# Three turns of tables for the expert sums, six row buffers, and scatters over 112 partitions

## Chip, cores and metric

The kernel runs on one core of a Trainium2 chip. The metric is device time in microseconds (us) for one execution; a time given as "the kernel's" is the median of several executions. All stretches and starts below are in us from the start of the profiled span.

## What is computed

One transformer layer over 2 x 1024 tokens of width 256: causal attention with rotary positions, a residual and a layer norm, then a mixture of experts with a shared expert, again a residual and a layer norm. The change touches only how the outputs of the routed experts come together with the rest. Cut to what matters:

```python
E, K, H, F = (64, 6, 256, 96);  CAP = 2 * (256 * K // E)          # 48 slots for each expert
def _routed_moe(x, topk_w, topk_ids, w_gate, w_up, w_down):
    order = jnp.argsort(topk_ids.reshape(-1));  se = flat_e[order];  tok = order // K
    pos = jnp.arange(Tn * K) - jnp.searchsorted(se, se, side='left')   # place within its expert
    valid = pos < CAP                                                   # later tokens are dropped
    buf = zeros((E, CAP + 1, H)).at[se, slot].set(x[tok])[:, :CAP]
    h = silu(einsum('ech,ehf->ecf', buf, w_gate)) * einsum('ech,ehf->ecf', buf, w_up)
    out = einsum('ecf,efh->ech', h, w_down)
    return segment_sum(out[se, pos] * valid * w, tok, num_segments=Tn)  # sum over a token's experts
x = layernorm(x + attention(x))
x = layernorm(x + routed_moe(x) + silu(x @ ws_gate) * (x @ ws_up) @ ws_down)
```

## The kernel before

**Attention and routing.** Up to about 990 us the kernel projects, attends and routes, tile by tile (16 tiles of 128 tokens). Every engine walks the same list of steps, `SEQ`, and waits on semaphores. For each tile the step `x1t` lets SyncE write zeros into the tile's rows of the sum tables (`blank_sums`, L576): all tables but the first, whose rows are written by step `sd` (L644), which stores the first layer norm's output plus the shared expert. The step `place` scatters each token's row into its six experts' slots (L729, GpSimd). Each expert has 64 slots (`HALF`) in `slot_rows`, of which at most 48 (`CAP`) are filled. SyncE also loads the experts' weights into 28 places (`HOMES`) as attention's memory comes free.

**Experts.** The 64 experts go in 32 pairs, one expert on partitions 0 to 63 and the other on 64 to 127, so that the slots in use are partitions 0 to 47 and 64 to 111. For pair `n` TensorE transposes the slots (L1038), multiplies by gate and up weights (L1048), transposes the hidden values (L1055) and multiplies by the down weights (L1062). ScalarE writes the result, times the routing weight of each slot, into row buffer `erow[n % EB]` (L879, `rows_out`), with `EB = 4`. GpSimd then issues one indirect DMA with an add (L742): each of the 128 partitions' rows of 1 KB is added to a row of the tables `sums` in HBM. An unused slot is directed to a spare row behind the tokens' rows.

**Tables and turns.** Two adds in flight must not touch the same row. So the two experts of a pair have a table each, and pairs alternate between two turns: `TURNS = 2`, `TABLES = 2 * TURNS = 4`. GpSimd issues pair `n` only when the pair `n - TURNS` has landed (`used(pool, erow_sent[n % TURNS], ...)`, L741), and ScalarE writes a row buffer again only when pair `n - EB` has landed (L878). ScalarE works in order, and `rows_out(n - 2)` stands behind `slots_in(n + 1)` and `gate_sig(n)`: a wait in it stops the inputs of later pairs too. The four pairs that have no place in `wexp` at first are loaded when `dn_ready` reaches 8, 12, 16 and 20 (L651), and the slots come in six chunks, the last three issued by ScalarE behind pairs 0, 6 and 12 (L892).

**Final sums.** When the last scatter of every turn has landed (L654), SyncE loads the tables, chunk by chunk (`FINAL = 8` chunks of 256 tokens, 256 KB for each chunk and table, L657). TensorE adds the tables of even chunks by matmuls with the identity (L1084), VectorE those of odd chunks by adds (L1340). Both wait for all tables of the chunk. VectorE then takes mean and variance (L1330, L1333), GpSimd the power (L750), ScalarE applies them (L899), and SyncE stores the chunk (L660).

Of the kernel before, what the change touches and what calls it, by code (L numbers as in the profile page):

```python
# [7 lines left out]
ALU = mybir.AluOpType  # L8
ACT = mybir.ActivationFunctionType
AX_X = mybir.AxisListType.X  # L10
F32 = mybir.dt.float32
# [4 lines left out]
P = 128  # L16
# [13 lines left out]
CAP = 2 * (256 * K // E)  # L30
PAIRS = E // 2
# [1 line left out]
SLOT_CUTS = (0, 2, 8, 14, 20, 26, PAIRS)  # L33
SLOT_CHUNKS = len(SLOT_CUTS) - 1
CHUNK_AT = {n: g for g, n in enumerate(SLOT_CUTS[:-1])}
EB = 4
TURNS = 2
TABLES = 2 * TURNS
HALF = P // 2
TOKENS = B * T  # L40
TABLE = TOKENS + P
# [4 lines left out]
FAR = 1.0e5  # L46
ABOVE, GONE = 1e30, -3e38
SLOTS = E * HALF
BLANKS = 4

UNITS = TILES * G
# [178 lines left out]
def build(nc, x, w_aq, w_ak, w_av, w_ao, gate_w, bias, w_gate, w_up, w_down, ws_gate, ws_up, ws_down,  # L230
# [4 lines left out]
    sums = nc.dram_tensor("sums", (TABLES * TABLE, M), F32, kind="Internal").ap()  # L235
# [3 lines left out]
    with ExitStack() as ctx:  # L239
        def sb(name, shape, dt, where=ctx):  # L240
            return where.enter_context(nc.sbuf_tensor(name, shape, dt))

        def sem(name):
            return ctx.enter_context(nc.semaphore(name))
# [6 lines left out]
        ones_bf = sb("ones_bf", [P, P], BF16)  # L251
        minus_half = sb("minus_half", [P, 1], F32)
        slots_left = sb("slots_left", [P, E], F32)
        row_base = sb("row_base", [P, PAIRS], F32)
        spare = sb("spare", [P, 1], F32)
        pool_cell = sb("pool_cell", [P, 1], F32)
        dve_cell = sb("dve_cell", [P, 1], F32)
# [90 lines left out]
        goal_u = sb("goal_u", [P, PAIRS], U32, exp)  # L348
        erow = sb("erow", [P, EB, M], F32, exp)
        exp.close()  # L350
# [85 lines left out]
        erow_ready = sem("erow_ready")  # L436
        erow_sent = [sem(f"erow_sent{n}") for n in range(TURNS)]
        fsum_added = sem("fsum_added")
# [60 lines left out]
        def used(eng, semaphore, n):  # L499

            if n > 0:
                eng.wait_ge(semaphore, n)
# [10 lines left out]
        def down_bank(n):  # L513
            return ring[:, n % 2, 0:M]
# [13 lines left out]
        def _(sp):  # L528
            def load_x(n):
                i = n % TILES  # L530
                sp.dma_start(x_sb[:, n % XB, :], xf[i * P:(i + 1) * P, :]).then_inc(x_loaded[n % XB], 16)

            load_x(0)
            for name in BLOCKS_IN_TURN:
                n = BLOCKS.index(name)
# [19 lines left out]
            def load_pair(n):  # L555
                k = n % HOMES
                for a, w in enumerate((w_gate, w_up)):
                    dst = wexp[:, k, 0:GATE_UP].rearrange("p (e a y) -> p e a y", e=2, a=2)[:, :, a, :]
                    sp.dma_start(dst, w[2 * n:2 * n + 2, :, :].rearrange("e (p c) f -> p e (c f)", c=MC)
                                 ).then_inc(experts_loaded[k], 16)  # L560
                sp.dma_start(wexp[0:F, k, GATE_UP:].rearrange("f (e m) -> f e m", e=2),
                             w_down[2 * n:2 * n + 2, :, :].rearrange("e f m -> f e m")
                             ).then_inc(experts_loaded[k], 16)
# [20 lines left out]
            for s in SEQ:  # L584
                if s[0] == "xt" and s[1] >= 1:
                    sp.wait_ge(xt_ready, s[1])
                    load_x(s[1] + 2)
                if s[0] == "xt" and 1 <= s[1] <= SLOTS // P // BLANKS:
                    n = s[1] - 1
                    sp.dma_start(slot_rows.rearrange("(p n) r -> p n r", p=P)[:, n * BLANKS:(n + 1) * BLANKS, :],  # L590
                                 blank[:, :].rearrange("p (a r) -> p a r", a=1).to_broadcast([P, BLANKS, ROW])
                                 ).then_inc(blank_stored, 16)
# [57 lines left out]
            for n in range(HOMES, PAIRS):  # L650
                sp.wait_ge(dn_ready, SLOT_CUTS[2] + 4 * (n - HOMES))  # L651
                load_pair(n)
            for n in range(TURNS):
                sp.wait_ge(erow_sent[n], 16 * (PAIRS // TURNS))  # L654
            for c in range(FINAL):
                for a in range(TABLES):
                    sp.dma_start(fsum[:, c, a, :], token_rows[a][:, c, :]).then_inc(fsum_loaded[c], 16)  # L657
# [7 lines left out]
        def _(pool):  # L665
            own = [0]

            def link(ins):

                own[0] += 1  # L670
                ins.then_inc(pool_own, 1)
                pool.wait_ge(pool_own, own[0])
# [3 lines left out]
                                    pattern=[[-1, P]], channel_multiplier=1))  # L676
# [7 lines left out]
                                    pattern=[[-1, P]], channel_multiplier=1))  # L684
# [3 lines left out]
                                    pattern=[[-1, P]], channel_multiplier=1))  # L688
# [6 lines left out]
            link(pool.memset(open_[:, :], ABOVE))  # L695
            link(pool.iota(slots_left[:, :], pattern=[[-HALF, E]], base=SLOTS, channel_multiplier=0,
                           allow_small_or_imprecise_dtypes=True))
            for e in range(2):
                link(pool.iota(row_base[e * HALF:(e + 1) * HALF, :], pattern=[[0, PAIRS // TURNS], [2 * TABLE, TURNS]],
                               base=e * TABLE, channel_multiplier=0, allow_small_or_imprecise_dtypes=True))  # L700
            link(pool.iota(spare[:, :], pattern=[[0, 1]], base=TOKENS, channel_multiplier=1,
                           allow_small_or_imprecise_dtypes=True))
# [2 lines left out]
            for s in SEQ:  # L705
                if s[0] == "proj" and s[2] != "V":

                    n = ROPE_AT[s[1:]]
# [14 lines left out]
                if s[0] == "place":  # L723
                    i = s[1]
                    if i == 0:
                        pool.wait_ge(blank_stored, 16 * (SLOTS // P // BLANKS))
                    pool.wait_ge(placed, i + 1)
                    for k in range(K):
                        pool.indirect_dma_start(  # L729
                            slot_rows[:, :], bass.IndirectOffsetOnAxis(ap=slot_u[:, i % 2, k:k + 1], axis=0),  # L730
                            row[:, i % 2, :], None, bounds_check=SLOTS - 1, oob_is_err=False
                        ).then_inc(scattered[i % 2], 16)
# [4 lines left out]
            for n in range(PAIRS):  # L737
                if n in CHUNK_AT:
                    pool.wait_ge(slots_known, CHUNK_AT[n] + 1)
                pool.wait_ge(erow_ready, n + 1)  # L740
                used(pool, erow_sent[n % TURNS], 16 * (n // TURNS))  # L741
                pool.indirect_dma_start(  # L742
                    sums[:, :], bass.IndirectOffsetOnAxis(ap=goal_u[:, n:n + 1], axis=0),
                    erow[:, n % EB, :], None, bounds_check=TABLES * TABLE - 1, oob_is_err=True, compute_op=ALU.add
                ).then_inc(erow_sent[n % TURNS], 16)


# [7 lines left out]
        def _(act):  # L755
# [9 lines left out]
            for s in SEQ:  # L765
                for name in HIGH_AT.get(s, []):
                    n = BLOCKS.index(name)
# [43 lines left out]
                if kind == "exp":  # L811
                    u, h = s[1:]
                    n = u * H + h
# [9 lines left out]
                if kind == "ptrans":  # L823
                    n = PT_AT[s[1:]]
# [47 lines left out]
            def rows_out(n):  # L872

                act.wait_ge(dn_ready, n + 1)
                if n in CHUNK_AT:
                    act.wait_ge(slots_known, CHUNK_AT[n] + 1)

                used(act, erow_sent[n % TURNS], 16 * ((n - EB) // TURNS + 1))  # L878
                act.activation(erow[:, n % EB, :], down_bank(n), ACT.Copy, scale=slot_w[:, n:n + 1]  # L879
                               ).then_inc(erow_ready, 1)  # L880

            for n in range(PAIRS + 2):
                if n == 0:
                    slots_in(0)
                if n + 1 < PAIRS:
                    slots_in(n + 1)
                if n < PAIRS:
                    gate_sig(n)
                if n >= 2:
                    rows_out(n - 2)  # L890
                if n in CHUNK_AT and 1 <= CHUNK_AT[n] < SLOT_CHUNKS - 2:
                    load_slots(CHUNK_AT[n] + 2)  # L892
# [196 lines left out]
        def _(dve):  # L1089
# [15 lines left out]
            def after(ins):  # L1105

                later(ins)
                settled()
# [5 lines left out]
            for s in SEQ:  # L1114
# [145 lines left out]
                if kind == "place":  # L1260
                    i = s[1]
                    read(dve, ("count", i))
                    with nc.allow_low_precision("at most one a tile"):
                        dve.tensor_tensor(taken[:, :], taken[:, :], chose[:, :], ALU.add)
                    after(dve.tensor_tensor(ahead[:, :], ahead[:, :], fits[:, :], ALU.mult))
                    after(dve.max(slot8[:, :], ahead[:, :]))
                    dve.tensor_scalar(slot_u[:, i % 2, :], slot8[:, :], -1.0, float(SLOTS), ALU.mult, ALU.add  # L1267
                                      ).then_inc(placed, 1)
# [110 lines left out]
```

## Time and profile before

| | us |
|---|---|
| median of 3 runs | 1127.45 (1126.43 to 1128.49) |
| the profiled execution: its time | 1126.55 |
| its span, first to last instruction | 1124.70 |
| start of the first scatter of the experts' sums | 1004.65 |
| start of the last scatter | 1085.84 |
| start of the first load of the tables | 1089.70 |
| start of VectorE's first add of the last chunk | 1115.49 |

The profiled execution is 0.90 us under the median. Of its time 1.85 us lies outside the span. Over the whole span TensorE is 90% busy, but that is an average over stages: in the last 120 us it is not, and the rows further down are read from these.

### The profile page before, as it was taken

Reading aid. Unit: us, or ns where it says so; the run is one execution under the profiler, and the core shown is the slowest. Engines: PE = TensorE matmul, PEld = TensorE weight load, DVE = VectorE, ACT = ScalarE, POOL = GpSimd, SP = SyncE. Lnnn points to the kernel's source line nnn. Section 1 sums busy time; section 2 is a strip of 40 time slices with the busy share of each in tenths; the row PEclk is TensorE's granted clock in tenths of the full one; section 3 lists DMA queues with packets and bytes.
Section 4 is the critical chain, followed back from the end, with each engine's and each line's share of the span. In section 5 each row is a group of like instructions: output and inputs, shape, how many; then the busy total and the mean of one; then the engine's idle time right before and its main releaser. Section 6 shows DMA issues by size and latency. Waiting matters only on the chain.

```text
span 1124.7 us, 16829 instructions
## 1 busy us (share of the span) xinstructions
PE 1017.0 (90%) x5312; PEld 731.9 (65%) x5312; DVE 562.6 (50%) x1533; ACT 518.7 (46%) x1147; POOL 363.4 (32%) x402
## 2 busy tenths in 40 slices
PE   6999998789999999999998899999999999657825
PEld 4888887566667776767666666777776676434512
DVE  5766765365554454443425675454535444323306
ACT  3333334454564556454543555464645645133312
POOL 6666665123322212103033313313021121035641
PEclk9999999799999999999999999999999999868868
DMA  7455233533321111111113323333211033968558
GB/s 230 163 180 183 105 117 108 163 91 106 95 63 62 53 56 49 38 43 51 34 44 98 101 80 95 112 104 100 65 39 52 26 92 91 245 178 175 80 100 315
DMA packets 99462, 117.57 MB, mean 105 GB/s; under 512 B 16065, under 2 KB 69173, under 8 KB 99376
## 3 DMA queue, kind: packets, MB, share of 16 engines
q1 hardware_dynamic: 76752, 87.65, 25.3%
q10 hardware_dynamic: 13408, 22.09, 6.5%
q0 software_dynamic: 9216, 6.76, 4.0%
q8 instruction: 44, 0.72, 0.3%
q14 instruction: 42, 0.34, 0.1%
HBM read 76.48 MB, written 53.35 MB: 115 GB/s over the span
## 4 chain that ended last, share of the span: by engine, by line
PE 75%; DMA 9%; DVE 6%; issue 4%; ACT 3%; SPq 2%; POOL 1%; ACTq 0%; POOLq 0%; DVEq 0%
PE o_ps L986 21%; PE s_ps L963 16%; PE ring L973 11%; PE ring L994 10%; DMA sums<-erow,goal_u 6%; PE s_ps L934 6%; PE ring L934 5%; PE s_ps L941 1%; SPq L657 1%; PE s_ps L966 1%; DVE neg_max L1150 1%; ACT probs L820 1%; DMA fsum<-sums 1%; PE o_ps L934 1%; PE ring L941 1%
## 5 line engine op out<-in xcount | busy, mean ns | idle before, releaser
L986 PE MATMUL o_ps<-pt,v 128*128 128x512 f32 x576 | 297.2, 598 | 3.9 <-DVE ot L1165 3.8
L828 ACT ACTIVATE pt<-ring 128x512 f32<-128x512 f32 x288 | 170.9, 594 | 252.1 <-PE ring L973 251.8
L963 PE MATMUL s_ps<-kt,qt_hi 128*128 128x512 f32 (+3 forms) x768 | 261.3, 422 | 3.5 <-issue 1.9
L1150 DVE TENSOR_REDUCE neg_max<-s_ps 128x1 f32<-128x128 f32 (+7 forms) x256 | 191.8, 753 | 135.8 <-PE s_ps L966 135.2
L820 ACT ACTIVATE probs<-s_ps,neg_max 128x128 f32<-128x128 f32 (+7 forms) x256 | 189.3, 740 | 110.2 <-DVE neg_max L1150 102.4
L718 POOL TENSOR_TENSOR qt_lo<-q_raw,qt_hi 128x512 fp32r<-128x512 f32 x64 | 81.2, 1270 | 474.1 <-ACT qt_hi L758 474.1
L963 PEld LDWEIGHTS s_ps<-kt,qt_hi 128*128 128x128 f32 x768 | 139.4, 194 | 79.4 <-issue 61.2
L973 PE MATMUL ring<-ident,probs 128*128 128x128 f32 x1152 | 176.2, 276 | 11.4 <-ACT probs L820 11.3
L973 PEld LDWEIGHTS ring<-ident,probs 128*128 128x128 f32 x1152 | 129.3, 142 | 56.8 <-issue 56.8
L963 PE MATMUL s_ps<-kt,qt_lo 128*128 128x512 f32 (+3 forms) x384 | 134.2, 350 | 0.0
L729 POOL DMA_INDIRECT slot_rows<-row,slot_u x96 | 94.5, 984 | 66.5 <-DVE slot_u L1267 39.7
L994 PE MATMUL ring<-wo,ot 128*128 128x256 f32 x512 | 113.1, 379 | 0.0
L994 PEld LDWEIGHTS ring<-wo,ot 128*128 128x128 f32 x512 | 97.1, 190 | 19.1 <-issue 6.7
L986 PEld LDWEIGHTS o_ps<-pt,v 128*128 128x128 f32 x576 | 87.8, 192 | 6.6 <-issue 6.4
L712 POOL TENSOR_TENSOR q_rot<-q_cos,q_sin 128x256 f32<-128x256 f32 x80 | 60.8, 760 | 63.0 <-DVE q_sin L1138 63.0
L963 PEld LDWEIGHTS s_ps<-kt,qt_lo 128*128 128x128 f32 x384 | 73.6, 192 | 8.3
L1165 DVE TENSOR_TENSOR ot<-o_ps,inv_row 128x512 f32<-128x512 f32 x64 | 44.1, 690 | 67.8 <-PE o_ps L986 62.7
L742 POOL DMA_INDIRECT sums<-erow,goal_u x32 | 49.3, 1542 | 48.0 <-ACT erow L879 25.2
L1173 DVE TENSOR_TENSOR y_sb<-ring,x_sb 128x256 f32<-128x256 f32 x16 | 6.8, 425 | 113.0 <-PE ring L994 113.0
L713 POOL TENSOR_TENSOR q_rot<-q_cos,q_sin 128x256 f32<-128x256 f32 x80 | 61.4, 768 | 0.0
L966 PE MATMUL s_ps<-causal_bf,ident_bf 128*128 128x128 bf16 x256 | 59.8, 233 | 0.0
L820 ACT ACTIVATION_READ_ACCUMULATOR probs<-s_ps,neg_max 128x1 f32 x256 | 50.4, 197 | 0.0
(182 smaller groups left out, 1283.7 us busy)
## 6 DMA issues: line engine op xcount, KB each, us to landing
q_rows<-q_out SPq DMA_DIRECT2D x64, 256.0 KB, 2.0
q_raw<-q_rows ACTq DMA_DIRECT2D x64, 256.0 KB, 2.7
inv_row<-inverses SPq DMA_DIRECT2D x64, 256.0 KB, 3.3
fsum<-sums SPq DMA_DIRECT2D x32, 256.0 KB, 6.9
sums<-blank SPq DMA_DIRECT2D x16, 384.0 KB, 2.8
wexp<-in_L_ffn_w_gate_dram SPq DMA_DIRECT2D x32, 192.0 KB, 3.9
wexp<-in_L_ffn_w_up_dram SPq DMA_DIRECT2D x32, 192.0 KB, 4.2
wexp<-in_L_ffn_w_down_dram SPq DMA_DIRECT2D x32, 192.0 KB, 5.0
```

The costliest lines, as they stand in the source:

```text
L713: pool.tensor_tensor(rot[:, :, 1, :], by_cos[:, :, 1, :], by_sin[:, :, 0, :], ALU.add).then_inc(rot_ready, 1)
L718: pool.tensor_tensor(qt_lo[:, u % 2, :], q_raw[:, u % QB, :], qt_hi[:, u % 2, :].bitcast(F32), ALU.subtract).then_inc(q_ready, 1)
L729: pool.indirect_dma_start(slot_rows[:, :], bass.IndirectOffsetOnAxis(ap=slot_u[:, i % 2, k:k + 1], axis=0), row[:, i % 2, :], None, bounds ...
L820: act.activation(probs[:, u % 2, h, 0:blocks(u) * P], s_ps[:, n % 2, score_cols(n)], ACT.Exp, bias=neg_max[:, n % 8:n % 8 + 1], accum_out= ...
L828: reader(act.activation(pt[:, n % PTB, :], bank(s), ACT.Copy), s)
L934: ins = pe.matmul(bank(s), (xt_hi, xt_lo)[xp][:, i % 2, c, :], (w_hi, w_lo)[wp][:, n, :, c, :], start=(c == 0 and xp == wp == 0), stop=(c ...
L963: pe.matmul(s_ps[:, n % 2, c + a:c + e], q[qp], k[kp][:, a:e], start=(qp == kp == 0), stop=(qp == 1 and not last))
L966: ins = pe.matmul(s_ps[:, n % 2, c + e - P:c + e], ident_bf[:, :], causal_bf[:, :], start=False, stop=True)
L973: ins = pe.transpose(bank(s)[:, h * P:(h + 1) * P], probs[:, u % 2, h, j * P:(j + 1) * P], ident[:, :])
L986: pe.matmul(o_ps[:, :], v_sb[i // NT][:, g, j, :], pt[:, n % PTB, :], start=(j == 0), stop=(j == blocks(u) - 1)).then_inc(pv_done, 1)
L994: ins = pe.matmul(bank(s)[:, 0:M], ot[:, h // H, (h % H) * P:(h % H + 1) * P], wo[:, h, :], start=(h == 0), stop=(h == G * H - 1))
L1150: dve.tensor_reduce(neg_max[:, n % 8:n % 8 + 1], s_ps[:, n % 2, score_cols(n)], AX_X, ALU.max, negate=True).then_inc(max_ready, 1)
```

## The change

`TURNS` goes from 2 to 3 and with it `TABLES` from 4 to 6; `EB` goes from 4 to 6. A pair's scatter covers 112 partitions, 0 to 111, in place of 128. The rest follows from it: `row_base` is rounded up to 33 columns so that its pattern repeats over three turns, and the wait ahead of the table loads counts each turn's own number of scatters (11, 11 and 10). Every loop over `TABLES` grows: `blank_sums` writes five tables in place of three, the blank of the spare rows six in place of four, the final loads are 48 in place of 32, TensorE adds six tables for each even chunk, and VectorE makes five adds in place of three for each odd one.

```diff
-EB = 4
-TURNS = 2
+EB = 6
+TURNS = 3
 TABLES = 2 * TURNS
...
 SLOTS = E * HALF
+USED = HALF + CAP
...
-        row_base = sb("row_base", [P, PAIRS], F32)
+        row_base = sb("row_base", [P, -(-PAIRS // TURNS) * TURNS], F32)
...
             for n in range(TURNS):
-                sp.wait_ge(erow_sent[n], 16 * (PAIRS // TURNS))
+                sp.wait_ge(erow_sent[n], 16 * len(range(n, PAIRS, TURNS)))
...
-                link(pool.iota(row_base[e * HALF:(e + 1) * HALF, :], pattern=[[0, PAIRS // TURNS], [2 * TABLE, TURNS]],
+                link(pool.iota(row_base[e * HALF:(e + 1) * HALF, :], pattern=[[0, -(-PAIRS // TURNS)], [2 * TABLE, TURNS]],
...
                 pool.indirect_dma_start(
-                    sums[:, :], bass.IndirectOffsetOnAxis(ap=goal_u[:, n:n + 1], axis=0),
-                    erow[:, n % EB, :], None, bounds_check=TABLES * TABLE - 1, oob_is_err=True, compute_op=ALU.add
+                    sums[:, :], bass.IndirectOffsetOnAxis(ap=goal_u[0:USED, n:n + 1], axis=0),
+                    erow[0:USED, n % EB, :], None, bounds_check=TABLES * TABLE - 1, oob_is_err=True, compute_op=ALU.add
                 ).then_inc(erow_sent[n % TURNS], 16)
...
-                used(act, erow_sent[n % TURNS], 16 * ((n - EB) // TURNS + 1))
+                used(act, erow_sent[(n - EB) % TURNS], 16 * ((n - EB) // TURNS + 1))
```

## Rows read from the trace of the kernel before

**Rows 1.** Chain that ended last, from 985 us on: shares by line.
```profile
by line: DMA sums<-erow,goal_u 49.7%; SPq L657 10.3%; issue 7.7%; DMA fsum<-sums 7.0%; ACT erow L879 4.5%; DMA slot_rows<-row,slot_u 3.0%; PE s_ps L1048 2.8%; DMA srow<-slot_rows 2.1%; POOL slot_rows L729 2.1%; POOL sums L742 1.7%; DVE fsum
```
**Rows 2.** Waits from 995 us on: who waited for whom, us in total, times, longest.
```profile
ACT erow L879 <- DMA sums<-erow,goal_u: 43.1, 24, 4.5
```
**Rows 3.** Timeline of GpSimd's scatters: start, us, instruction, idle before it.
```profile
1004.65 1.56 POOL L742 DMA_INDIRECT sums<-erow,goal_u  x1 [14.59 <-DVE dve_cell L1291]
...
1056.03 1.54 POOL L742 DMA_INDIRECT sums<-erow,goal_u  x1 [1.26 <-ACT erow L879]
...
1079.29 1.54 POOL L742 DMA_INDIRECT sums<-erow,goal_u  x1 [1.22 <-ACT erow L879]
...
1081.13 1.54 POOL L742 DMA_INDIRECT sums<-erow,goal_u  x1 [0.30 <-ACT erow L879]
1083.91 1.54 POOL L742 DMA_INDIRECT sums<-erow,goal_u  x1 [1.24 <-DMA sums<-erow,goal_u]
```
**Rows 4.** The chain again, in order: a scatter's time from its start to landing.
```profile
1015.05 6.86 DMA sums<-erow,goal_u
...
1033.49 5.66 DMA sums<-erow,goal_u
...
1079.29 3.81 DMA sums<-erow,goal_u
```
**Rows 5.** Timeline of the gate and up matmuls of single pairs, at either clock.
```profile
1007.37 0.88 PE L1048 MATMUL s_ps<-wexp,sxt 128*64 128x192 f32 x8
...
1009.09 0.88 PE L1048 MATMUL s_ps<-wexp,sxt 128*64 128x192 f32 x8
...
1022.87 1.55 PE L1048 MATMUL s_ps<-wexp,sxt 128*64 128x192 f32 x8 [3.06 <-issue]
...
1026.01 1.56 PE L1048 MATMUL s_ps<-wexp,sxt 128*64 128x192 f32 x8
```
**Rows 6.** DMA queues, 1004.6 to 1056: packets, MB, share of 16 engines (q0 is GpSimd's).
```profile
q0 software_dynamic: 2513, 2.30, 36.8%
q10 hardware_dynamic: 2329, 2.96, 18.8%
q1 hardware_dynamic: 3008, 2.36, 16.2%
```
**Rows 7.** The same for 1060.6 to 1083.9, where only scatters run.
```profile
q0 software_dynamic: 1449, 1.32, 52.2%
```
**Rows 8.** GpSimd's two kinds of scatter by line: duration ns min/median/max, first and last start.
```profile
L742 POOL DMA_INDIRECT sums<-erow,goal_u x32: 1532/1539/1570, 1004.7 to 1085.8; - x32
...
L729 POOL DMA_INDIRECT slot_rows<-row,slot_u x96: 967/972/1214, 253.0 to 989.1; - x96
```
**Rows 9.** Timeline of the final sums: issue of the loads, first use of some chunks.
```profile
1089.70 16.55 SPq L657 DMA_DIRECT2D fsum<-sums  x32
1095.86 9.47 PE L1084 MATMUL ring<-fsum,ident 128*128 128x512 f32 x16 [18.16 <-DMA fsum<-sums]
...
1104.69 0.69 DVE L1340 TENSOR_TENSOR fsum<-fsum 128x512 f32<-128x512 f32 x1 [0.37 <-DMA fsum<-sums]
...
1115.49 0.69 DVE L1340 TENSOR_TENSOR fsum<-fsum 128x512 f32<-128x512 f32 x1 [0.67 <-DMA fsum<-sums]
...
1117.09 0.69 DVE L1340 TENSOR_TENSOR fsum<-fsum 128x512 f32<-128x512 f32 x1
```
**Rows 10.** DMA from 1108 to 1115: all queues.
```profile
DMA packets 1494, 2.72 MB, mean 389 GB/s; under 512 B 169, under 2 KB 169, under 8 KB 1493
```
**Rows 11.** VectorE's waits for `inv_row`, 200 to 990: us in total, times, longest.
```profile
DVE ot L1165 <- DMA inv_row<-inverses: 3.5, 2, 2.5
```
**Rows 12.** Windows: PE, PEld, DVE, ACT, POOL busy, clock, DMA share, GB/s.
```profile
985.00:990.00 5.00, 0.40 (x2) 0.11 (x1) 0.48 (x2) 0.46 (x2) 3.83 (x4) 0.50 0.54 146
```

**Rows 13.** Windows of the scatters' stretch in which the clock was down, first and last of three.
```profile
1022.70:1027.80 5.10, 4.93 (x27) 3.16 (x27) 1.51 (x6) 1.84 (x8) 3.07 (x2) 0.50 0.45 56
...
1056.00:1060.60 4.60, 4.44 (x27) 2.74 (x27) 1.51 (x6) 1.89 (x8) 3.08 (x2) 0.63 0.48 52
```

## Prediction

> **What bounds the kernel now.** I read the chain that ended last first, and only its part behind attention, since the change leaves attention's work alone except for the blanks. From 985 us to the end, half of the chain is the DMA of the scatters with add, and the loads of the tables follow with 7.0% as a DMA and 10.3% as their issue by SyncE [rows 1]. TensorE's lines are 3% there. So two stretches matter: the 32 scatters, from 1004.65 to 1089.70, and the final sums, from 1089.70 to the end.
>
> In the first stretch ScalarE waits 43.1 us in total for scatters to land before it may write a row buffer [rows 2]. But the buffers are not what ends last. Take the quiet end of the stretch. Pair 28's scatter starts at 1079.29 and lands 3.81 us later, at 1083.10 [rows 4]; pair 30, of the same turn, starts at 1083.91, which is 0.8 us after that landing, with its row long written [rows 3]. Two scatters thus cost 3.8 + 0.8 = 4.6 us, one 2.3 us. Where no turn is waited for, the next scatter starts 1.84 us after the last (1079.29 to 1081.13), of which 1.54 us is GpSimd's own work and 0.30 us idle. TensorE, when nothing holds it and at the full 2.4 GHz, starts a pair every 1.72 us (1007.37 to 1009.09) [rows 5]. So the turn is the bound, GpSimd the next one at 1.84, TensorE the third at 1.72.
>
> The stretch has two halves. Up to pair 18 (1056.03) the last weights and slots are loaded beside the scatters: 18 intervals in 51.4 us, 2.85 us each, with landings of up to 6.86 us [rows 3, 4]. From there 13 intervals take 29.8 us, 2.29 us each. With the last landing (3.86 us) this makes 85.05 us.
>
> In the second stretch the DMA engines are the bound: VectorE's first add of the last chunk waits for its tables, at 1115.49 [rows 9], and just before that the engines move 389 GB/s [rows 10].
>
> **The third turn, quiet half.** A scatter now waits for the one three back, so the turn allows one in (3.8 + 0.8) / 3 = 1.53 us. GpSimd's 1.84 us takes over. What 112 partitions do to its 1.54 us no row shows. The slot scatters, also over 128 partitions, take 0.97 us [rows 8], so a part is certainly not the rows' transfer; between no effect and 112/128 of the whole lies 0 to 0.19 us, and at 1.65 us TensorE's 1.72 would be the bound. I take 1.80, near the no-effect end, because both kinds of scatter are flat in their durations (967 to 972 ns though fewer and fewer slots of later tiles are valid), which speaks for a large fixed part. 13 x 1.80 = 23.4 us in place of 29.8: a gain of 6.4 us (5.9 to 7.4).
>
> **The third turn, loaded half.** Here the DMA engines have a say. They spend 36.8% of 51.4 us on scatters, 18.9 us, and 35.0%, 18.0 us, on weights and slots [rows 6]. A scatter is 128 packets of rows and 16 more (1449 packets in some ten scatters [rows 7]), so 112 rows take 128/144 of it, 16.8 us. The sum of 34.8 us for 18 scatters is a floor of 1.93 us each, if the engines are never idle. The other end is a stretch in which all landings are like the longest: (6.86 + 0.8) / 3 = 2.55 us. A landing of 5.66 us, a middling one of this half, gives 2.15 us. I take 2.2, as bursts leave gaps between them: 39.6 us in place of 51.4, a gain of 11.8 us (5.5 to 16.6). That the buffers hold is no cost: six of them let ScalarE, and with it the input of later pairs, run six pairs ahead of landing, where a scatter lands about two starts after its own.
>
> The Trainium skill, in "DMA: Bandwidth & Descriptors", section "Why a DMA increments its semaphore by 16 and not by 1", says that a DMA runs on the largest number of engines up to 16 that divides its outermost size. 112 is 16 x 7, so by it each engine has 7 rows in place of 8 and none has more; if it were otherwise, the engine with 8 rows would set the landing and the scatters' share would stay 18.9 us, 0.1 us more for each scatter. No row here can show which.
>
> **The final sums.** 16 more loads of 256 KB are 4.19 MB, at 389 GB/s 10.8 us [rows 10]. By the chunks' own times: the first chunk is used 6.2 us after the first issue, the fourth is in at 1104.69 and the eighth at 1115.49, so 2.9 us for each early chunk of 1 MB and 2.70 for each later one [rows 9]; half as much again for all of it, with 2 us of the first as latency, gives 2.1 + 3 x 1.47 + 4 x 1.35 = 11.9 us. I take 11.3 (10.8 to 11.9). SyncE does not bind: 16.55 / 32 = 0.52 us for an issue against 0.67 us for 256 KB. Behind the last landing VectorE makes two adds more; the three there start at 1115.49 and end at 1117.78, 0.76 each, so 1.5 us. TensorE's two additional matmuls for each even chunk lie beside the loads (it has 8.1 us for two chunks; six tables at twice the earlier pace of loads are about 5.6 us). In all +12.8 us, with nothing to cover it.
>
> The Trainium skill, in the same page's section "Where 436 GB/s comes from", names some 358 GB/s as the limit of HBM for one core. The trace shows more, 389 GB/s, and decides; by the skill's figure the additional loads would be 11.7 us, inside my bounds.
>
> **The blanks.** 16 blanks grow from 384 to 640 KB each (three tables' rows to five), and what is queued behind them on SyncE is the inverses of the next unit and its `inv_row`. VectorE waits for `inv_row` only twice, 3.5 us in all [rows 11]. TensorE sets the pace of attention, so I cost these at nothing; if that cover were gone, 256 KB at half of the 389 GB/s is 1.3 us, for the first tile or two some 2 us. The last blank goes out at 977.5 behind the weights, and from 985 on the engines are at 54% [rows 12]: the backlog grows by about 1 us and has drained before the last slot scatter, at 989.1 [rows 8], needs them. The blank of the spare rows and the wider `row_base` lie ahead of it all. I put +0.3 us (0 to 2).
>
> **The sum.** -6.4 - 11.8 + 12.8 + 0.3 = -5.1 us on the profiled execution's 1126.55 us: 1121.4. The median is 0.90 us above the profiled one: 1122.3.
>
> **Rivals.** *The loads are absorbed.* The DMA engines' gaps fill, the loaded half runs near its floor, and the smaller scatters shorten GpSimd's part: 16 + 7 - 12.5 gives -10.5, about 1117, down to 1115. For it speaks that engines were at 72% in that half; against it that a chunk of slots and a pair's weights go out at about the same time, which no queue spreads.
> *Three in flight land later.* If the add of one scatter delays the next one's, or the bursts catch three scatters in place of two, the turn stays the bound. The final sums cost 12.8 us, which is 0.41 us for each of 31 intervals; the change loses from a mean interval of 2.62 - 0.41 = 2.21 us on. With landings of 6.86 us throughout the loaded half and of 6 in the quiet one (2.27 us) the gain is 5.5 + 0.3, and the time is 1135; nearer at hand is a loaded half of 2.5 and a quiet half of 2.1: 6.4 + 2.5 - 13.1 is +4.2, 1132. Against it: in the quiet half the engines are only 52% busy with scatters [rows 7], 1.2 us for each of ten, less than the 1.84 us between two starts.
> *TensorE takes over.* After a wait of 3.06 us a pair takes 3.1 us (1022.87 to 1026.01) [rows 5]; the granted clock is 0.50 there, the level of 1.2 GHz, and there are three such windows [rows 13]. Every such drop costs some 2 pairs x 1.3 us. Two or three of them with no rows in reserve take the gain down to nothing, 1125 to 1129. Against it: with shorter waits there should be fewer drops than the present three, not more.
> *It doesn't do what it says.* If GpSimd's wait isn't the bound but ScalarE's, six buffers give the gain alone. That gives the same time; the time doesn't tell them apart, an experiment would.
>
> **How the numbers follow.** Forecast (1119 to 1125) 0.50; loads absorbed (1114 to 1119) 0.20; TensorE or a mixture with about no gain (1125 to 1129.5) 0.18; three in flight land later (over 1129.5) 0.12. A measurement of this kernel can tell 0.2%, 2.3 us, from no change. That puts faster at 0.71, within 0.2% (1125.2 to 1129.7) at 0.18 and slower at 0.11. The bounds of the terms span 1115 to 1132; the range 1115 to 1129 leaves out a little under 2 in 10.
>
> **What would show it.** Right: scatters that start every 1.8 us in the quiet half with GpSimd's idle at 0.3 us, first scatter to first table load about 67 us, table loads of about 37 us up to the last chunk's first add, five adds there. Wrong: scatter starts further apart than 2.2 us in the mean; landings over 5.5 us with only scatters in flight; a granted clock of 0.5 over more of the stretch; a GpSimd instruction of the scatter under 1.45 us (then the rows count). The forecast falls if attention ends later, which the start of the first scatter (1004.65) shows.

## The result, and the profile after

The changed kernel takes 1119.67 us (median of 7 runs, 1117.05 to 1123.18) where the kernel before takes 1126.43 us in the runs beside it: a ratio of 0.9935, with a 95% interval of 0.9913 to 0.9956. The medians are 6.8 us apart, and the ratio makes it 7.3 us. The profiled execution took 1121.47 us, 5.1 us less than that of before, and its span is 1119.7 us, 5.0 us less.

Split at four instants, the two profiled executions differ like this (all in us; "behind" is from VectorE's first add of the last chunk to the end):

| | before | after | difference |
|---|---|---|---|
| up to the first scatter | 1004.65 | 1006.96 | +2.3 |
| first scatter to first table load | 85.05 | 64.83 | -20.2 |
| first table load to first add of the last chunk | 25.79 | 37.20 | +11.4 |
| behind | 9.21 | 10.71 | +1.5 |

The first line is not the change's, as far as the traces can tell. In the eight kernels of the table below, whose attention is the same work but for the blanks, the first scatter starts anywhere between 1002.42 and 1006.96 us. Nor does it start later with more blanks: over all fourteen kernels with a trace it starts at 1004.8 us in the mean of the ten with six tables and at 1005.4 in the mean of the four with four. Between the two executions here, 0.7 us of the difference are there at 23 us: the six matmuls of the second projection take some 0.39 us each in the one and 0.63 in the other (the first of the six 0.47 and 0.77). The granted clock reads 1.00 there in both, but 0.63 us is also what matmuls of the same line take at 185.6 to 189 us of the kernel before, where it reads 0.51. Another 1.6 us come between 180 and 210 us, at the handover from projections to attention, where the granted clock is below full in both (0.82 and 0.76). The other three lines belong to the change, and they come to -7.3 us, which fits the medians and the ratio.

The scatters after, from the timeline of GpSimd (start, duration, instruction, idle before it; it answers to [rows 3]):

```profile
1006.96 1.51 POOL L743 DMA_INDIRECT sums<-erow,goal_u  x1 [14.77 <-DVE dve_cell L1292]
...
1024.30 1.45 POOL L743 DMA_INDIRECT sums<-erow,goal_u  x1 [2.78 <-ACT erow L880]
...
1044.10 1.46 POOL L743 DMA_INDIRECT sums<-erow,goal_u  x1 [0.30 <-ACT erow L880]
1047.00 1.45 POOL L743 DMA_INDIRECT sums<-erow,goal_u  x1 [1.45 <-issue]
1048.76 1.46 POOL L743 DMA_INDIRECT sums<-erow,goal_u  x1 [0.30 <-issue]
...
1066.36 1.46 POOL L743 DMA_INDIRECT sums<-erow,goal_u  x1 [0.30 <-issue]
1068.12 1.46 POOL L743 DMA_INDIRECT sums<-erow,goal_u  x1 [0.30 <-issue]
```

From 1047.00 to 1068.12 twelve intervals are 1.76 us each, and the idle time is the 0.30 us that stood between two scatters already before. GpSimd does nothing but issue: it is the bound there now. Up to pair 18 (1044.10) 18 intervals take 37.14 us, 2.06 each.

The waits from 995 us on (who waited for whom: us in total, times, longest) answer to [rows 2], and the chain from 985 us on to [rows 1]:

```profile
ACT erow L880 <- DMA sums<-erow,goal_u: 6.3, 10, 1.3
```

```profile
by line: issue 21.8%; SPq L658 17.6%; PE s_ps L1049 11.6%; DMA fsum<-sums 7.3%; PE ring L1063 5.9%; PE s_ps L1039 4.0%; POOL sums L743 3.1%; DMA slot_rows<-row,slot_u 2.9%; POOL slot_rows L730 2.7%; DMA sums<-erow,goal_u 2.6%; DVE fsum L134
```

ScalarE's 43.1 us of waits are down to 6.3, and the scatters' DMA is 2.6% of the chain where it was half. The table loads (SPq L658) are up from 10.3 to 17.6%. TensorE stands there now with 21% in three lines, but that is no sign that it binds the scatters. The chain comes to TensorE through the start of pair 18's scatter at 1044.10, which it puts down to a row written at 1043.29. ScalarE writes 32 rows in order, and that one is the 22nd, pair 21's; pair 18's own was written 5.5 us before its scatter:

```profile
1038.08 0.47 ACT L880 ACTIVATE erow<-ring,slot_w 128x256 f32<-128x256 f32 x1 [0.58 <-PE ring L1063]
...
1043.29 0.47 ACT L880 ACTIVATE erow<-ring,slot_w 128x256 f32<-128x256 f32 x1 [0.25 <-DMA sums<-erow,goal_u]
```

Counted in the same way, only the rows of pairs 0 to 2 are written just before their scatters, 0.8 to 0.9 us before the start. From pair 3 on the row lies ready for at least 1.27 us, from pair 8 on for at least 3.8.

Windows of the changed kernel (PE, PEld, DVE, ACT, POOL busy, granted clock, DMA share, GB/s): the loaded half, the quiet half, the table loads, and behind them.

```profile
1006.90:1044.10 37.20, 36.70 (x313) 24.11 (x315) 17.31 (x75) 22.96 (x63) 26.31 (x19) 1.00 0.85 196
1044.10:1068.10 24.00, 14.63 (x123) 8.69 (x118) 6.69 (x29) 8.62 (x24) 18.91 (x13) 0.88 0.57 64
1071.80:1109.00 37.20, 23.54 (x45) 9.64 (x46) 17.43 (x50) 4.00 (x8) 4.19 (x6) 0.80 1.00 360
1109.00:1119.70 10.70, 1.51 (x4) 0.38 (x2) 6.06 (x19) 3.99 (x8) 1.38 (x2) 0.72 0.32 123
```

In the loaded half TensorE is 99% busy, its granted clock is 1.00 (2.4 GHz), and it runs ahead of the scatters; before, the clock fell toward 1.2 GHz three times [rows 13]. The table loads fill the DMA engines. The end of that stretch, and what VectorE does with the last chunk (it answers to [rows 9]):

```profile
1071.79 27.54 SPq L658 DMA_DIRECT2D fsum<-sums  x48
...
1108.99 0.69 DVE L1341 TENSOR_TENSOR fsum<-fsum 128x512 f32<-128x512 f32 x1 [2.33 <-DMA fsum<-sums]
...
1109.79 0.68 DVE L1341 TENSOR_TENSOR fsum<-fsum 128x512 f32<-128x512 f32 x1
...
1110.59 2.14 DVE L1341 TENSOR_TENSOR fsum<-fsum 128x512 f32<-128x512 f32 x3
```

Five adds, all behind the last load: 1108.99 to 1112.73.

### The profile page after: what moved, and what is told of

Same layout as the page of the kernel before. It is cut to its first block, busy times and chain, and to the rows that moved or that the text cites. A ratio compares the mean times of both kernels' runs of the same rounds, so it can differ in the third digit from the quotient of the medians.

```text
span 1119.7 us, 16883 instructions
## 1 busy us (share of the span) xinstructions
PE 1020.4 (91%) x5328; PEld 734.2 (66%) x5328; DVE 567.8 (51%) x1541; ACT 522.5 (47%) x1147; POOL 361.4 (32%) x402
## 4 chain that ended last, share of the span: by engine, by line
PE 78%; DVE 6%; issue 6%; DMA 4%; SPq 3%; ACT 2%; POOL 1%; ACTq 0%; POOLq 0%; DVEq 0%
PE o_ps L987 21%; PE s_ps L964 16%; PE ring L974 11%; PE ring L995 9%; PE s_ps L935 6%; PE ring L935 5%; SPq L658 2%; PE s_ps L1049 1%; PE s_ps L942 1%; PE s_ps L967 1%; DVE neg_max L1151 1%; ACT probs L821 1%; DMA fsum<-sums 1%; PE o_ps L935 1%; PE ring L942 1%
## 5 line engine op out<-in xcount | busy, mean ns | idle before, releaser
L974 PE MATMUL ring<-ident,probs 128*128 128x128 f32 x1152 | 175.7, 275 | 11.5 <-ACT probs L821 11.3
L743 POOL DMA_INDIRECT sums<-erow,goal_u x32 | 46.7, 1459 | 30.7 <-DVE dve_cell L1292 14.8
```

The costliest lines, as they stand in the source:

```text
L974: ins = pe.transpose(bank(s)[:, h * P:(h + 1) * P], probs[:, u % 2, h, j * P:(j + 1) * P], ident[:, :])
```

## The experiments

My theory: the turn (the wait for the scatter two back) was the bound, the third turn takes it away and leaves GpSimd's issue as the next one, and the two further tables cost about 12.8 us of loads and adds. The rivals: ScalarE's wait for row buffers was the bound, the smaller scatters carry the gain, the price is elsewhere. "The stretch" is the time from the first scatter to the first table load.

The stretches of all profiled executions, in us (the first scatter's own start is left out of them, as it moves by itself; the last column is from there to the end):

| kernel | turns, tables, buffers, rows | to first table load | of it up to pair 18 | table loads | behind | all |
|---|---|---|---|---|---|---|
| before | 2, 4, 4, 128 | 85.05 | 51.38 | 25.79 | 9.21 | 120.05 |
| tables_only | 2, 6, 4, 128 | 85.58 | 52.23 | 36.68 | 10.67 | 132.93 |
| buffers_only | 2, 4, 6, 128 | 83.17 | 48.94 | 25.93 | 9.24 | 118.34 |
| rows_only | 2, 4, 4, 112 | 80.36 | 48.16 | 26.41 | 9.25 | 116.02 |
| turns_only | 3, 6, 4, 128 | 69.22 | 41.30 | 37.18 | 10.68 | 117.08 |
| after_128 | 3, 6, 6, 128 | 67.81 | 39.99 | 37.05 | 10.71 | 115.57 |
| after_eb4 | 3, 6, 4, 112 | 64.52 | 37.67 | 37.31 | 10.65 | 112.48 |
| after | 3, 6, 6, 112 | 64.83 | 37.14 | 37.20 | 10.71 | 112.74 |

### The third turn alone

The edit, from the changed kernel:

```diff
-EB = 6
+EB = 4
-USED = HALF + CAP
+USED = P
```

> The changed kernel with four row buffers and 128 partitions, so only the third turn and its two tables are left. If the turn was the bound: the scatters' stretch (first scatter to first table load) falls from 85 us to 67 to 70, with GpSimd's starts 1.84 us apart where only scatters run, and the final sums cost 13 us more, so 2 to 5 us faster than the kernel before. If the four row buffers were the bound: the stretch stays above 80 us and the kernel is 8 to 13 us slower.

Measured: ratio to the kernel before 0.9985 (0.9971 to 0.9999), median 1124.30 against 1126.92 us. The stretch is 69.22 us, 15.8 less than before. GpSimd, by line (duration ns min/median/max; then what ended its idle time, us and times):

```profile
L743 POOL DMA_INDIRECT sums<-erow,goal_u x32: 1533/1541/1570, 1002.4 to 1067.9; - x32
...
  ACT erow L880: 6.9, 6
  issue: 5.9, 19
  DMA sums<-erow,goal_u: 4.9, 6
```

The turn was the bound: with four buffers and 128 partitions as before, the intervals in the quiet half are 1.86 us in the mean in place of 2.29. But of the 15.8 us the two tables take back 12.9 (measured below), which leaves 2.9 us. By the ratio it is 1.7 us, just under the 2 to 5 that I expected: the third turn alone would have been a change of 0.15%.

### The buffers alone

The edit, from the kernel before:

```diff
-EB = 4
+EB = 6
```

> The kernel before with six row buffers in place of four, two turns, four tables, 128 partitions. If the turn is the bound: the stretch stays within 2 us of 85, because a scatter still waits for the one two back; 0 to 2 us faster. If ScalarE's 43 us of waits for row buffers were the bound: the waits fall and 10 us or more come out of the stretch.

Measured: ratio 0.9998 (0.9981 to 1.0014). The stretch is 83.17 us: 2.4 us less in its loaded half, 0.6 more in the quiet one.

```profile
ACT erow L879 <- DMA sums<-erow,goal_u: 35.6, 23, 4.0
```

That settles the rival of the buffers as the bound of the kernel before. The long wait in the waits view was real, and a deeper ring took 7.5 us of it away, yet GpSimd still stood waiting for the scatter two back. The views put most of its waits down to ScalarE's rows (`<-ACT erow`), which misleads: one landing releases both engines. Pair 21's scatter starts at 1062.83 and lands 4.03 us later, by the chain:

```profile
1062.83 4.03 DMA sums<-erow,goal_u
```

At that landing, 1066.86, ScalarE writes a row, and 0.8 us behind it the scatter of pair 23 starts:

```profile
1066.93 0.47 ACT L879 ACTIVATE erow<-ring,slot_w 128x256 f32<-128x256 f32 x1 [1.79 <-DMA sums<-erow,goal_u]
...
1067.67 1.54 POOL L742 DMA_INDIRECT sums<-erow,goal_u  x1 [1.16 <-ACT erow L879]
```

Counted in order, that row is pair 27's; pair 23's own had been ready for 9.7 us. ScalarE's wait was the echo of the turn on another engine.

### The rows alone

The edit, from the changed kernel:

```diff
-EB = 6
-TURNS = 3
+EB = 4
+TURNS = 2
```

> The kernel before with scatters over 112 partitions, two turns, four buffers. If a turn's time is GpSimd's part plus the landing: GpSimd's part is 1.46 us in place of 1.54 and the landing (3.8 us from the start) some 0.2 us shorter, so 4.4 us for two scatters in place of 4.6, 2 to 4 us faster. If the rows carry the change's gain: 7 us or more faster, with the landing 0.5 us shorter.

Measured: ratio 0.9973 (0.9955 to 0.9991), 3 us; its stretch is 4.7 us shorter, and from the first scatter to the end it is 4.0 us.

```profile
L743 POOL DMA_INDIRECT sums<-erow,goal_u x32: 1449/1452/1513, 1005.1 to 1081.9; - x32
```

GpSimd's part falls from 1539 to 1452 ns, 87 ns for 16 rows, and two scatters of one turn take 4.4 us in the quiet half (28.63 us for 13 intervals) in place of 4.6. At hardly any price this is as much as the third turn alone gave, net, or more: 4.0 against 3.0 us from first scatter to end; the intervals of the two ratios overlap.

### The rows undone

The edit, from the changed kernel:

```diff
-USED = HALF + CAP
+USED = P
```

> The changed kernel with scatters over 128 partitions again, six buffers and three turns. If GpSimd is now the bound: starts are 1.84 us apart in place of 1.76, so the stretch is 31 x 0.08 = 2.5 us longer than the changed kernel's 64.8 us and the kernel 4 to 5 us faster than the kernel before in place of 7. If the DMA engines bound the loaded half: 4 us or more are lost, most of them before pair 18.

Measured: ratio 0.9961 (0.9946 to 0.9976), 4.4 us; the stretch is 67.81 us, 3.0 longer than the changed kernel's. 31 x 0.087 = 2.7 of them are GpSimd's time for an instruction, which is exposed now that GpSimd is the bound; its idle time adds up to about the same in both. It does not lie in the same places, though. Nearly all of the difference comes before pair 18 (39.99 against 37.14), where GpSimd's time explains only 18 x 0.087 = 1.6, and in the quiet half the changed kernel has one gap of 1.45 us (above), behind the last late weights.

Against turns_only, which differs by the buffers alone and ran beside it, this kernel is faster: 67.81 against 69.22 us of stretch, medians of 1122.00 and 1124.30. The intervals of the two ratios just overlap (0.9946 to 0.9976 and 0.9971 to 0.9999). So with three turns of 128 rows two more buffers may be worth 1 to 3 us.

### The buffers undone

The edit, from the changed kernel:

```diff
-EB = 6
+EB = 4
```

> The changed kernel with four row buffers in place of six (three turns, 112 partitions). If the buffers only cover bursts of loads: the quiet half keeps 1.76 us a scatter, the loaded half loses 1 to 4 us, so 1 to 4 us slower than the changed kernel. If the buffers are no part of it: the same within 0.5 us. If they carry the gain: 8 us or more slower.

Measured: ratio 0.9902 (0.9885 to 0.9919) to the kernel before, whose runs beside it have a median of 1129.56 us, 3 us over those beside the changed kernel; so I go by the stretches, one trace of each. The one to the first table load is 64.52 us against 64.83, the whole of it 112.48 against 112.74. With 112 rows and three turns no gain of the two further buffers shows.

### The tables alone

The edit, from the kernel before:

```diff
-TABLES = 2 * TURNS
+TABLES = 6
```

All six tables are blanked, loaded and added, the last two hold zeros.

> The kernel before with six tables blanked, loaded and added, of which the scatters still use four: two turns, four buffers, 128 partitions. This measures the price by itself. By my sum: 11.3 us more from first table load to VectorE's first add of the last chunk, 1.5 us more behind it, nothing in attention; 12 to 14 us slower in all. If the blanks or the start are not covered: the first scatter starts 1 to 3 us later too and it is 14 to 17 us slower.

Measured: ratio 1.0089 (1.0071 to 1.0108), 10 us by the ratio, 11.1 between the medians, 12.9 us by the traces from first scatter to end (132.93 less 120.05). The profile has 10.9 us in the loads, 1.5 us behind them and 0.5 us in the scatters' stretch:

```profile
1092.35 27.32 SPq L657 DMA_DIRECT2D fsum<-sums  x48
```

```profile
1129.03 0.69 DVE L1340 TENSOR_TENSOR fsum<-fsum 128x512 f32<-128x512 f32 x1 [2.01 <-DMA fsum<-sums]
```

The median ratio is below my 12 to 14; its interval reaches 12.2 us. The terms lie where the sum had them, and no cost of the blanks or of the start shows: the first scatter, at 1006.77 us, is within the spread given above.

### The late weights left out

Pairs 28 to 31 compute with the weights of pairs 0 to 3; nothing is loaded for them beside the scatters.

The edit, from the changed kernel:

```diff
             for n in range(HOMES, PAIRS):
                 sp.wait_ge(dn_ready, SLOT_CUTS[2] + 4 * (n - HOMES))
-                load_pair(n)
+                pass
...
-                pe.wait_ge(experts_loaded[n % HOMES], 48 * (n // HOMES + 1))
+                pe.wait_ge(experts_loaded[n % HOMES], 48)
```

> The changed kernel without the loads of the last four pairs' weights; pairs 28 to 31 compute with those of pairs 0 to 3, so their outputs are not the reference's. If the loads beside the scatters are what lifts the loaded half from 1.76 to 2.2 us a scatter: most of the excess of 18 x 0.4 = 8 us goes that is not the slots' own, 3 to 6 us, and landings over 5 us are fewer. If TensorE or its clock is the cause: the gaps stay, and less than 1.5 us goes.

Measured: ratio 0.9905 (0.9879 to 0.9931), again to the kernel before at 1129.56 us; the loaded half is 36.93 us against 37.14, and the stretch 63.61 against 64.83, 1.2 us less. The other 1.0 us lie behind pair 18. There the changed kernel has its one gap, before pair 19, which waits for pair 16's scatter; that one starts at 1040.58, beside the last weights:

```profile
1039.76 0.37 SPq L560 DMA_DIRECT2D wexp<-in_L_ffn_w_gate_dram  x1
```

Without these loads the idle time before pair 19 is 0.43 us in place of 1.45. The number is in my second case, under 1.5 us, but the cause that I named with it, TensorE, is not it: the rows of pairs 8 and 13 lay ready 3.1 and 5.5 us before their scatters. So both cases of my expectation were wrong, and so was the weight that I gave to these loads. The gaps that are left:

```profile
1017.38 1.45 POOL L743 DMA_INDIRECT sums<-erow,goal_u  x1 [0.41 <-issue]
1021.37 1.45 POOL L743 DMA_INDIRECT sums<-erow,goal_u  x1 [2.54 <-DMA sums<-erow,goal_u]
...
1028.44 1.45 POOL L743 DMA_INDIRECT sums<-erow,goal_u  x1 [0.31 <-issue]
1032.75 1.45 POOL L743 DMA_INDIRECT sums<-erow,goal_u  x1 [2.86 <-DMA sums<-erow,goal_u]
```

These two, of 2.5 and 2.9 us, before pairs 8 and 13, are most of what this half has above 1.76 us a scatter (4.8 of 5.3 us). Pair 8 waits for pair 5, which starts at 1013.76, and pair 13 for pair 10, which starts at 1024.89. At these times ScalarE issues a chunk of slots, which lands in 6.4 us:

```profile
1013.87 0.37 ACTq L856 DMA_DIRECT2D srow<-slot_rows  x1
...
1024.75 0.37 ACTq L856 DMA_DIRECT2D srow<-slot_rows  x1
```

```profile
srow<-slot_rows ACTq DMA_DIRECT2D x2, 972.0 KB, 6.4
```

That leaves the slots' loads as what lifts this half. It is argued from the coincidence in time and not shown: loading them earlier was not tried.

### The third turn retired early

The edit, cut, from the changed kernel (`EARLY` is tables 4 and 5; the tables of `fsum` lie one behind the other, so that these two fall where no weights are in use any more; the waits and `row_base` go by `TURN_OF`):

```diff
+LAST_OF_THREE = 24
+TURN_OF = [n % TURNS for n in range(LAST_OF_THREE)] + [n % 2 for n in range(PAIRS - LAST_OF_THREE)]
...
+            sp.wait_ge(erow_sent[2], 16 * TURN_OF.count(2))
+            for c in range(FINAL):
+                sp.wait_ge(erow_ready, LAST_OF_THREE + 1 + c if LAST_OF_THREE + 1 + c < PAIRS else PAIRS)
+                for a in EARLY:
+                    sp.dma_start(fsum[:, a, c, :], token_rows[a][:, c, :]).then_inc(fsum_loaded[c], 16)
```

> The changed kernel, but the third turn takes its last pair at 23; pairs 24 to 31 use two turns, and the third turn's two tables are loaded, two chunks' worth of 512 KB after each of these pairs, beside the last scatters. If the engines' spare time can be used: 10.8 us of loads leave the final sums, the last eight scatters lengthen from 14 to 20 to 24 us, and the kernel is 1 to 5 us faster than the changed one. If loads lengthen two turns' landings as they did in the loaded half of the kernel before (2.85 us a scatter and more): the last eight take 25 us or more and nothing is gained, or up to 3 us lost.

Measured: from first scatter to the end 113.97 us, 1.2 more than the changed kernel; ratio 0.9930 (0.9907 to 0.9953), beside the kernel before at 1129.56 us. That is my second case (the last eight take 25.4 us). The loads filled the engines (their share is 0.98 from 1053 to 1068 us), and the scatters, with only two turns, came late:

```profile
1056.10 1.45 POOL L754 DMA_INDIRECT sums<-erow,goal_u  x1 [1.28 <-ACT erow L892]
1060.90 1.45 POOL L754 DMA_INDIRECT sums<-erow,goal_u  x1 [3.35 <-ACT erow L892]
1065.03 1.45 POOL L754 DMA_INDIRECT sums<-erow,goal_u  x1 [2.68 <-DMA sums<-erow,goal_u]
1068.92 1.45 POOL L754 DMA_INDIRECT sums<-erow,goal_u  x1 [2.43 <-DMA sums<-erow,goal_u]
```

Intervals of 3.9 to 4.8 us in place of 1.76. The final sums then became shorter by 7.9 us (43.66 us from the last scatter's start to the end, against 51.58), less than the 10.8 of the loads, because VectorE, once it had begun, no longer waited for chunks at all: it had become the bound there.

### Tables loaded turn by turn, and the last chunk table by table

The edit of early_loads, cut, from the changed kernel (`load_sums` issues one load; those that are done are left out of the loop that follows), and under it that of stream_last, cut, where each table of the last chunk has a semaphore of its own, one left over from the start. `both` has the two edits together, and two_turns_both has them with two turns, four tables, four buffers and 112 partitions:

```diff
+            sp.wait_ge(dn_ready, PAIRS)
+            for n in range(PAIRS - TURNS, PAIRS):
+                sp.wait_ge(erow_sent[n % TURNS], 16 * (n // TURNS + 1))
+                for c in range({3: 4, 2: 2, 1: 0}[PAIRS - n]):
+                    for a in (2 * (n % TURNS), 2 * (n % TURNS) + 1):
+                        load_sums(c, a)
```

```diff
                 for a in range(1, TABLES):
+                    if c == FINAL - 1:
+                        dve.wait_ge(w_loaded[a], 32)
```

> The changed kernel, but SyncE does not wait for all turns before the first table load: when the turn of pair 29 has landed it loads that turn's two tables for four chunks, then those of pair 30's turn for two chunks, then, with the last turn, the rest. If the final loads are bound by the DMA engines alone: they begin 3.5 us earlier, beside two scatters only, and the last chunk is complete 2 to 3.5 us earlier. If, as with eight scatters over two turns, loads hold up the scatters that they run beside: the last scatter lands 3 us later and nothing is gained.

> The changed kernel with a semaphore for each table of the last chunk, so that VectorE adds a table as soon as it has landed and not when all six have. If VectorE's five adds are exposed behind the last load, as the sum has it: four of them (0.72 us each) move beside the loads, and from the last load's landing to the end it is 2.5 to 3 us less; 2 to 3 us faster. If the loads bunch at the end, so that the six tables land together: under 1 us.

> The changed kernel with the earlier table loads and the semaphore for each table of the last chunk. If both terms are real and independent: the sum of the two, 4.5 to 6 us faster than the changed kernel, 11 to 13 us faster than the kernel before.

> Two turns, four tables, four buffers and 112 partitions, with both of these edits. If the third turn's net gain (about 20 us of scatters with the rows, 5 without, against 12.8 us of tables) stays what it was: 3 to 5 us slower than the kernel with three turns and both edits. If the edits take back part of the tables' price, which only three turns pay in full: 5 to 6 us slower.

Measured side by side (the kernel before has 1127.32 us there; the two rows in brackets are from their own traces, and the changed kernel did not run beside these):

| kernel | median | ratio, 95% interval | last scatter's start to the end |
|---|---|---|---|
| early_loads | 1118.22 | 0.9908, 0.9889 to 0.9927 | 47.95 |
| stream_last | 1118.85 | 0.9918, 0.9898 to 0.9938 | 48.93 |
| both | 1116.19 | 0.9892, 0.9871 to 0.9913 | 47.56 |
| two_turns_both | 1123.00 | 0.9968, 0.9952 to 0.9983 | 39.72 |
| (the changed kernel) | | | 51.58 |
| (rows_only) | | | 39.23 |

From the last scatter to the end each edit gives about what it should, 3.6 and 2.7 us, but the two together 4.0 and not 6.3, less than the 4.5 to 6 that I expected. VectorE's waits of `both` from the first load on show why:

```profile
DVE fsum L1356 <- DMA fsum<-sums: 24.6, 1, 24.6
DVE fstats L1341 <- PE ring L1095: 3.3, 1, 3.3
DVE nmr L1335 <- POOL frs L761: 0.7, 1, 0.7
```

After its first wait, and another one for TensorE's first sums (L1095), VectorE never waits for a load again, where the changed kernel has 31.7 us in 4 waits. Its own work, 6.07 us for two chunks (it begins the mean and variance of chunks 4 and 6 at 1101.36 and 1107.43), is now the bound to the end. `both` is the fastest of all, 11 to 12 us below the kernel before; that it is faster than either edit alone is within their intervals, and its interval (0.9871 to 0.9913) just touches the changed kernel's (0.9913 to 0.9956).

With two turns the same edits give nothing (39.72 against 39.23). In both cases the earlier loads let VectorE wait for TensorE's first sums (3.3 us in place of none with three turns, 3.15 in place of 1.2 with two), so that it begins the first mean and variance later, 22.5 us behind the last scatter's start in place of 19.8 with three turns, 18.8 in place of 16.8 with two. What they take away is the waits for loads behind that point: 6.4 us with three turns (2.07, 1.96 and 2.33), but only 1.4 with two (0.70 and 0.66). Why TensorE's first sums come later was not looked into. `both`, with its third turn and six buffers, is 6.8 us faster than two_turns_both, more than the 3 to 6 that I expected.

## Why the prediction was right

- **What bounds.** Right: the turn, not the buffers (buffers_only 0.9998), and after it, in the quiet half, GpSimd's issue with its 0.30 us of idle between scatters.
- **Quiet half.** I took 1.80 us a scatter; it is 1.76 in steady state. The step from 128 to 112 rows was bounded at 0 to 0.19 us on GpSimd and measured 0.087, so I stood too near to the no-effect end: the flat durations of the slot scatters, on which I rested, are flat in the number of valid rows, not of partitions. The half as a whole took 24.0 us for 13 intervals, a gain of 5.8 us and so just under my 5.9 to 7.4, because of the gap before pair 19.
- **Loaded half.** I took 2.2 us (1.93 to 2.55); it is 2.06, a gain of 14.2 in place of 11.8 us. The landing of 5.66 us on which this rested was no middling one: the chain shows nine in this half, with a median of 4.84 us, and only one is longer. I had counted weights and slots alike as engine time; taking the weights away changed this half by 0.2 us, so a floor from summed engine time was not what bound. Single bursts fit what is left, but were not tested by themselves. Scatters of 112 rows land in 3.6 us where those of 128 rows take 3.8. That fits the rule of the Trainium skill ("DMA: Bandwidth & Descriptors", section "Why a DMA increments its semaphore by 16 and not by 1"), by which each of 16 engines has 7 rows in place of 8; it does not show it, as no row has the engines singly.
- **Final sums.** 11.3 + 1.5 us forecast, 11.4 + 1.5 measured, and 10.9 + 1.5 with the tables alone. The rate from the later chunks was the right one:

```profile
DMA packets 1490, 2.72 MB, mean 388 GB/s; under 512 B 166, under 2 KB 166, under 8 KB 1489
```

  That is 1101 to 1108 of the changed kernel, against 389 before [rows 10]. The Trainium skill gives some 358 GB/s as HBM's limit for one core ("DMA: Bandwidth & Descriptors", section "Where 436 GB/s comes from"); this stretch exceeds it as well.
- **Blanks.** +0.3 us forecast; nothing stands out of the spread of the first scatter's start, 1002.42 to 1006.96 us, and a cost of this size could not be seen in it.
- **The sum.** -5.1 us forecast, -5.1 us between the profiled executions, but that agreement is partly luck: the terms of the change gave -7.3, and 2.3 us of chance in attention hid two of them. Against the medians (-6.8) I was 1.7 us short, from the loaded half. As a time, 1122.3 us were forecast and 1119.67 measured: 2.6 us, of which 1.0 is the kernel before, whose median was 1127.45 us when I forecast and 1126.43 beside the changed kernel.
- **The rivals.** TensorE did not take over: its clock is 1.00 in the loaded half, and from pair 3 on the rows lay ready before their scatters could start. Three scatters in flight did not land later where only scatters run: 3.62 us for the last one, 3.5 in the median of eleven in no_late_weights from 1048 us on. Beside loads they did in one case: the longest landing in after_128's chain is 8.03 us, against 6.86 before. The loads were absorbed in part. (In the sum for three in flight, 6.4 + 2.5 - 13.1 is -4.2, a loss of 4.2 us; the time of 1132 that I drew from it is right.) The mechanism of that rival did appear in the experiment that loads tables beside eight scatters on two turns.

## What to carry to other kernels

When an engine's longest wait is for a resource that another wait governs (here row buffers, freed by scatters that wait for each other), deepen the governing one; more buffers mostly move the wait (here 35.6 us of it were left of 43.1, and the time was the same). Price a parallel copy of an accumulator by what it costs to merge it: here two more tables took back 12.9 of 15.8 us, and trimming unused rows from each transfer, at no price that showed, was worth as much as the net of that or more. Once a bound is removed look at the next one for small costs that were covered before: 0.09 us an instruction became 3 us.

## What the runs showed of the hardware

- The time of GpSimd for an indirect DMA with add depends on the partitions: 1539 ns at 128, 1452 to 1455 ns at 112, some 5.4 ns each; an estimate from these two: the rest, about 0.85 us, would be fixed if that slope held throughout, which was not tried.
- A scatter of 112 rows lands 3.5 us (median of eleven, no_late_weights) to 3.6 us (the changed kernel's last) after its start, with the scatters issued 1.76 us apart; the DMA engines are then 57% busy in the changed kernel.
- Attention's end moves by 4.5 us between kernels whose attention is the same but for the blanks (1002.42 to 1006.96 for the first scatter). Between the two compared here 0.7 us of it come at the start, where six matmuls take 0.63 us each in one execution and mostly 0.39 in the other.
